# Graph attention on one core: gathers of the seventh block on wait for TensorE's spread and sums of the slot three steps back

## The reference

```python
q = (x @ Wq + bq).reshape(n_nodes, HEADS, HEAD_DIM)
k = (x @ Wk + bk).reshape(n_nodes, HEADS, HEAD_DIM)
v = (x @ Wv + bv).reshape(n_nodes, HEADS, HEAD_DIM)
scores = jnp.sum(q[dst] * k[src], axis=-1) * scale + (edge_attr @ We + be)
max_s = jax.ops.segment_max(scores, dst, num_segments=n_nodes)
e = jnp.exp(scores - max_s[dst])
denom = jax.ops.segment_sum(e, dst, num_segments=n_nodes) + 1e-10
weighted = ((e / denom[dst])[:, :, None] * v[src]).reshape(n_edges, -1)
agg = jax.ops.segment_sum(weighted, dst, num_segments=n_nodes)
out = _layernorm(x + agg @ Wo + bo, axis=-1)
```

## Time and profile before

| | us |
|---|---|
| three runs | 2611.83, 2622.75, 2625.79 |
| median | 2622.75 |
| the profiled execution | 2600.53 |
| its span, from the first to the last instruction | 2598.6 |
| PE busy | 1413.5 |
| DVE busy | 1352.6 |
| ACT busy | 430.0 |
| POOL busy | 1498.5 |
| mean granted clock of TensorE | 0.657 of full speed |

### The profile page before, as it was taken

The page is one execution under the profiler, slowest core; times in us unless marked ns, Lnnn a source line. Parts: engine busy times, 40 slices in busy tenths (PEclk is TensorE's granted clock), DMA queues, the critical chain, the costliest instruction groups (busy, mean ns, idle before and its releaser), DMA issues.

```text
span 2598.6 us, 31022 instructions
## 1 busy us (share of the span) xinstructions
PE 1413.5 (54%) x9783; PEld 946.5 (36%) x9783; DVE 1352.6 (52%) x3156; ACT 430.0 (17%) x1439; POOL 1498.5 (58%) x1572
## 2 busy tenths in 40 slices
PE   5265455555554554546555545555554555555557
PEld 4133243333333343333333333334333333333334
DVE  4254454545554554555555545545454555455556
ACT  1011111111111111111111111111111111111112
POOL 4725565555656566655656555656665665656540
PEclk7556675666666666666666766656676667566767
DMA  6423333333333334333433333343333333333320
GB/s 250 149 75 101 118 104 115 105 102 121 108 117 104 117 103 122 106 119 101 124 99 118 106 100 119 105 122 102 121 104 119 101 121 104 119 105 112 113 84 7
DMA packets 115162, 288.47 MB, mean 111 GB/s; under 512 B 45909, under 2 KB 53856, under 8 KB 107960
## 3 DMA queue, kind: packets, MB, share of 16 engines
q0 software_dynamic: 74624, 203.26, 26.5%
q1 hardware_dynamic: 37628, 76.52, 9.0%
q10 hardware_dynamic: 2748, 6.69, 0.7%
HBM read 274.69 MB, written 11.67 MB: 110 GB/s over the span
## 4 chain that ended last, share of the span: by engine, by line
another core or an unknown queue 36%; PE 32%; DVE 20%; issue 9%; ACT 2%; DVEq 0%; ACTq 0%; DMA 0%
PE q_banks L1215 11%; PE ps_a L1252 7%; DVE prod L833 4%; DVE score L844 4%; PE ps_e L1227 2%; PE ps_t L1192 2%; PE ps_s L1273 2%; DVE wv L854 2%; DVE run_fwd L896 1%; PE ps_a L1294 1%; PE ps_t L1198 1%; PE ps_s L1279 1%; PE ps_a L1304 1%; DVE cand L890 1%
## 5 line engine op out<-in xcount | busy, mean ns | idle before, releaser
L508 POOL DMA_INDIRECT kv_buf<-kv_table,src_i x1536 | 1469.0, 956 | 1020.5 <-DVE wv L854 582.8
L1215 PE MATMUL q_banks<-q_blk,hots 64*128 64x128 f32 x3128 | 417.6, 406 | 462.9 <-issue 225.2
L598 ACT ACTIVATE hots<-ps_t 128x512 f32<-128x512 f32 x377 | 225.1, 597 | 1974.8 <-PE ps_t L1198 962.6
L1215 PEld LDWEIGHTS q_banks<-q_blk,hots 64*128 64x128 f32 x3128 | 319.9, 278 | 582.3 <-issue 562.4
L833 DVE TENSOR_TENSOR prod<-q_banks,kv_buf 128x512 f32<-128x512 f32 (+1 forms) x392 | 269.0, 686 | 379.2 <-remote 251.4
L854 DVE TENSOR_TENSOR wv<-kv_buf,ps_w 128x512 f32<-128x512 f32 (+1 forms) x392 | 265.8, 679 | 356.5 <-remote 333.9
L1252 PE MATMUL ps_a<-wv,hots 128*64 128x136 f32 x3128 | 375.4, 378 | 5.4 <-ACT wv L639 4.8
L1294 PE MATMUL ps_a<-sums_sb,carry_from 128*1 128x136 f32 x112 | 34.1, 406 | 530.3 <-DVE sums_sb L964 524.1
L844 DVE TENSOR_REDUCE score<-prod 128x32 f32<-128x512 f32 (+1 forms) x392 | 267.3, 682 | 7.7
L1252 PEld LDWEIGHTS ps_a<-wv,hots 128*64 128x64 f32 x3128 | 239.2, 183 | 68.2 <-issue 52.1
L1294 PEld LDWEIGHTS ps_a<-sums_sb,carry_from 128*1 128x1 f32 x112 | 4.8, 81 | 551.9 <-DVE sums_sb L964 545.4
(11 more groups left out here) (155 smaller groups left out, 1403.4 us busy)
## 6 DMA issues: line engine op xcount, KB each, us to landing
edge_f<-in_edge_blk SPq DMA_DIRECT2D x55, 1024.0 KB
kv_buf<-kv_table,src_i POOLq DMA_INDIRECT x1536
kv_table<-kv_buf ACTq DMA_DIRECT2D x12, 512.0 KB, 2.8
xt_blk<-in_x_t SPq DMA_DIRECT2D x114, 32.0 KB
out<-y_out SPq DMA_DIRECT2D x114, 32.0 KB
kv_buf<-in_x_perm SPq DMA_DIRECT2D x5, 512.0 KB
codes<-code_table SPq DMA_DIRECT2D x108, 10.5 KB
code_table<-kv_buf SPq DMA_DIRECT2D x1, 1344.0 KB
```

The lines of the kernel that those rows point to most:

```text
L508: pool.indirect_dma_start(kv_buf[:, b % NBUF, t, :], None, kv_table, bass.IndirectOffsetOnAxis(ap=src_i[:, column:column + 1], axis=0)).th ...
L598: one = act.activation(hots[:, v % 2, :, :].rearrange("p k n -> p (k n)"), ps_t[:, :], ACT.Relu, bias=1.0)
L1215: one = pe.matmul(ps_q[j][:, k * D:(k + 1) * D], hots[own, (v - 1) % 2, 0, k * P:(k + 1) * P], q_blk[own, b % QBUF, :], start=True, stop=True)
```

## The change

From the seventh block on (`HELD` = 6) a step's gathers wait twice more. The first pair of gathers of step q waits until `s_byedge` has reached q - 2: the spread of step q - 3 is done, which PE works in slot q - 3. The second pair waits until `s_summed` has reached q - 15: the sums of step q - 16 are done, which PE works in the same slot, after the spread. The wait for the weighing stays.

```diff
     XAHEAD = 3
+
+    HELD, AHEAD = 6, 3
     assert T <= SLOT * QUAD
...
                 for g, (t0, t1) in enumerate(STEP[b]):
                     if b >= NBUF:
                         pool.wait_ge(s_weighted, steps_over(b - NBUF, t1))
+                    q = FIRST[b] + g
                     for t in range(t0, t1):
                         column = FIRST_TILE[b] + t
+                        if b >= HELD and t == t0:
+                            pool.wait_ge(s_byedge, q - AHEAD + 1)
+                        if b >= HELD and t == t0 + 2:
+                            pool.wait_ge(s_summed, q - AHEAD - SLOT - LAG)
                         pool.indirect_dma_start(
                             kv_buf[:, b % NBUF, t, :], None, kv_table,
```

## The result

The changed kernel takes **2485.86 us** (median of four runs, 2477.36 to 2486.70). The kernel before, run beside it, takes 2621.30 us (four runs, 2611.83 to 2625.79). The ratio is **0.9481**, with a 95% interval of 0.9447 to 0.9514: 5.2% faster. The forecast was 2480 us. The profiled execution of the changed kernel took 2485.12 us, with a span of 2483.3 us.

A forecast was written before the change was run, and what follows sets the result against it. Bound: PE's completions, held while gathers queue at 1.42 us each. Stage 1982 + 47 + 55 = 2084 us against 2225, a gain of 141; 2622.75 - 141 = 2482, say 2480 us, range 2390 to 2640.

The forecast's parts named there:

- Service: From the seventh block on, gathers hold PE's completions like a queue serving one per 1.42 us: 1982 us for 1396.
- Restarts: When the queue empties, POOL's next gather follows PE's release by 0.27 us, 175 times: 47 us.
- The fold: At a block's second slot the spread comes late, behind DVE's add: 2.17 us at half of 51 blocks, 55 us.
- Waits at no cost on POOL: The 700 added waits on POOL cost 0, at most 210 us at 0.30 us each.
- Shorter lead at no cost: Gathers standing three slots ahead instead of up to nine still land in time for DVE: cost 0.
- The passage: POOL holds back some 19 us at the seventh block; the part after the last gather shortens by the same: 0 net.
- the border of 3 us: PE completions due within 3 us of a gather run's start pass at once; later ones are held.
- Rule against row: The page says DMA never contends with compute engines; the prediction trusted the trace, where PE's completions stand still during gathers.
- Pairs alone keep PE free: Rival: pauses after pairs reset the grace, nothing is held, POOL's pace counts: 1745 us stage, 2143 us total; chance 0.07.
- The gathers are not the cause: Rival: PE's completions are late for another reason, so pacing gathers brings nothing: about 2620 us; chance 0.07.
- The queue empties before PE has executed what POOL waits for: Slower rival: the next spread must first be made, 2.56 us at each of 175 releases: 2828 us; chance 0.18.
- Too late data: Rival: DVE waits for gathers' landings, up to 2 us at each block, +100 us: 2580 us; chance 0.08.

The follow-up runs named there:

- the kernel woken by DVE: Changed kernel with both waits for PE replaced by one for DVE's weighing three slots back, before a step's first gather only: 2636.87 us, ratio 1.0107.
- the lead of eight: Changed kernel with its waits looking eight slots back instead of three: 2023.27 us, ratio 0.9992 where nothing is held; 2486.72 us, ratio 0.9482 where completions are held.
- the first group: Runs on one chip where no completions were held: four variants of the changed kernel beside the kernel before, which took 2024.63 us there.
- a lead of one: Changed kernel with a step's pairs waiting for the spread and sums of the slot before, instead of three back: 2520.91 us, ratio 0.9647.
- two variants of it: Changed kernel with waits eight slots back (0.9992 in this group, 0.9482 elsewhere), and changed kernel without the wait for sums (0.9997 and 0.9617).

## Why the prediction was right

**Mechanism and sum.** The forecast was a stage of 2084 us and a gain of 141 us on it; the stage took 2098 us and gained 127. The parts:

- *Service, 1396 x 1.42 = 1982 us.* Held. The distances of runs of eight and ten differ by 2.82 us for two gathers, ten narrow gathers gave 1.43 us each, and twelve in the kernel woken by DVE 17.15 us in all.
- *Restarts.* Expected were 175 of 0.27 us (47 us) and 55 us at the fold, 102 us together; measured are 210 restarts and 116 us. I counted six to eight gathers a run; 6, 8 and 10 came, and 35 runs of only two. By the means, the runs of eight come to 91 x (11.68 - 11.36) = 29 us, those of ten to 26 x 0.42 = 11, those of six to 54 x 0.60 = 32 and those of two to 35 x 1.18 = 41. An ordinary restart, counted beyond the service, is thus 0.3 to 0.45 us, somewhat above the 0.27 expected, and the short runs carry the rest.
- *The fold, 55 us.* Not where I put it, so that the sum came out near is luck. POOL waits for the block's second slot at the two pairs of a block's fifth step. Only 27 restarts stand there, with 14 us beyond the service, about as much as elsewhere. The places with the most are the pairs that wait for the third and the fourth slot: 65 restarts with 54 us. At some of these PE has not yet made the spread when the queue is empty (lines below).
- *Waits at no cost on POOL.* Right: the gap between gathers of a run is still 0.30 us and their busy time unchanged. The upper bound of 210 us did not come near, and the lead of eight in the first group issued without a pause.
- *Shorter lead at no cost.* Right for three: eight gives the same (0.9482 to 0.9481). With one it costs 1.7 points.
- *The passage, taken as 0.* The start moved by 28 us where 19 were expected, the end came 16 us closer instead of 19: 12 us of loss that the sum did not have. With the 14 us of the stage that makes the 26 us by which the gain on the span (115) fell short of 141.
- *The median.* The difference of the two medians is 135 us, near the forecast; the profiled run of before lay 0.8% under its median (2600.53 to 2621.30), that of after on its own. The hit to 0.2% owes a part of itself to that.

**A step that was mis-sized.** The free pace of PE was read from 158 to 180 us as 22 us a block. It is 27.3 us (3.90 a slot): those early slots of the earlier trace rows have hardly any gathers, but hardly any weighings and sums either (three weighings and the sums of two steps for eight products). I did not see this since I counted products only, not what else a full slot does. The number entered the sum only at the passage (six slots of 3.90 are 23 us, nearer to the 28 found) and the margins of two rivals. 27.3 is still under the 39.8 us of service that a block of 28 gathers needs, so the bound was the right one.

**Holding as the prediction described it.** That everything held comes free at the end of the queue was too strong. I compared the end of the match's records with the start of ACT's copy, for copies before which ACT was idle. In the changed kernel, of matches due within 3 us of a run's start 104 of 116 reached ACT within 0.3 us, of those due 3 to 5 us after it 19 of 65, of later ones none of 149; before, 134 of 139, 6 of 84 and 7 of 110. So the border of 3 us holds. But 62 of the 65 and 39 of the 149 came before the run's service was over: a completion is late by some microseconds, not always until the end.

**Rule against row.** In four groups of runs the row holds: 2606 to 2623 us with all gathers, 1754.9 with none from the seventh block on (one group), and what is still held at the end of a run comes 1.42 us a gather after its start. The Trainium skill, page "SBUF — State Buffer", section "Who interferes with whom", says that a DMA never contends with a compute engine. What is seen late here are PE's completions; whether its accesses to SBUF are late too no run shows, so the rule may be true of the ports and still mislead on the time. In the first group of runs nothing contradicts it: PE kept up with gathers that never paused.

**The rivals.** *Pairs alone keep PE free*: the premise is true (1750.42 us with a pair a slot), but with four gathers a step the pairs join into runs of 6 to 10, as was argued against it. *The gathers are not the cause*: falls by 1754.9 us. *The queue empties before PE has executed what POOL waits for*: falls as the rule, since POOL's pauses are 1.88 us on average and end at PE; of a pause behind eight gathers 0.30 us are the ordinary gap and 1.36 us the time by which their service outlasts their issue, so no 2.56 us can be in it besides. It does happen behind some of the 35 runs of two, which together cost 41 us:

```profile
364.64 0.60 ACT L605 ACTIVATE hots<-ps_t 128x512 f32<-128x512 f32 x1 [8.34 <-remote]
...
364.97 0.94 POOL L515 DMA_INDIRECT kv_buf<-kv_table,src_i  x1 [1.75 <-remote]
...
366.21 0.94 POOL L515 DMA_INDIRECT kv_buf<-kv_table,src_i  x1 [0.30 <-issue]
...
367.44 1.22 PE L1222 MATMUL q_banks<-q_blk,hots 64*128 64x128 f32 x8
...
369.43 0.95 POOL L515 DMA_INDIRECT kv_buf<-kv_table,src_i  x1 [2.27 <-PE q_banks L1222]
```

The copy is released at 364.64 and POOL issues a pair, whose service is over at 364.97 + 2.84 = 367.81. PE dispatches the spread that POOL waits for only at 367.44, and POOL goes on at 369.43. *Too late data*: only at a lead of one.

**What would show it.** The signs came: gaps that end at PE, runs of six to ten for the most part, a release at 1.42 to 1.47 us a gather (11.72 for eight), the next gather 0.17 us behind it in the cycle shown (the median of 0.57 us is more than the 0.3 named), a block in 2098 / 51 = 41 us, as expected, and gathers' busy time unchanged.

## What to carry to other kernels

Where one engine's transfers delay another's completions, look at the first instruction after each release: if the issuing engine is woken by a third engine that must first work, wake it by the delayed engine's own signal; a restart of 0.55 instead of 1.56 us was worth 5% here, with no instruction less. Size such a queue by the distance between the starts of runs of different lengths, whose slope is the service and whose rest is the restart, and check it on the releases themselves. Before building on it, take the transfers out once (869 us here) and measure the kernel before beside it every time, since the same kernel may run where there is no queue at all.

## What the runs showed of the hardware

- **The holding is not always there.** One and the same kernel took 2024.63 us in one group of runs (19 runs, 2021.37 to 2027.74) and 2598.69 to 2634.58 us in all others. In the first, 28 gathers a block at POOL's 35.1 us held nothing. The changed kernel itself was not run there; two variants of it, worth 5.2 and 3.8% elsewhere, were worth 0.1 and 0.0% there. What differs is open; no experiment touched it.
- **The unpaced gathers ahead of the blocks hold completions too**: the first product starts at 140 to 145 us instead of 65 to 66, within four microseconds of the end of the service of 56 gathers (140.5 to 142.8 us at 1.42 us each). No kernel of the study paces them, so what that would bring is open.
- **A gather's service is 1.42 us with rows of half the length too** (14.27 us for ten, at a DMA share of 0.24 instead of 0.39). Which resource it shares with PE's completions stays open.
- **A pair with a pause is free, a long run is not** (one run of half the gathers): 462 gathers in 900 us left PE and DVE at the 747 and 756 us of busy time that they have without any; 600 gathers in 900 us, in runs, leave them at this:

```profile
600.00:1500.00 900.00, 556.27 (x3657) 368.26 (x3657) 498.43 (x1159) 158.92 (x532) 573.33 (x600) 0.61 0.39 118
```
